# Moving the output sum, the row normalisation and three steps of algebra to other places in the engines' orders

## What is computed

```python
xn = layernorm(x)
# attention: l2-normed Q and K over the rows, all products linear, so a 256x256 matrix per batch
s = xn + gamma * (value_sum + Q^T (K V^T)) * tailor_sum
# feed-forward, every operand in blockwise FP4 (blocks of 16, scale = max|.|/6, rounded to a grid)
gate = fp4(xn) @ fp4(w_gate).T          # 704 wide
y    = fp4(xn) @ fp4(w_up).T
h    = silu(gate) * y
f    = fp4(h) @ fp4(w_down).T
out  = x + s * silu(f)
```

## Time and profile before

| | |
|---|---|
| median of 3 runs | 636.19 us |
| the profiled execution | 638.52 us, span 636.7 us |
| mean granted TensorE clock | 0.973 of full speed |
| DVE busy | 566.0 us (89%) |
| PE busy | 557.4 us (88%) |
| ACT busy | 411.6 us (65%) |
| POOL busy | 273.4 us (43%) |

### The profile page before, as it was taken

The page is one execution under the profiler, slowest core; times in us unless marked ns, Lnnn a source line. Parts: engine busy times, 40 slices in busy tenths (PEclk is TensorE's granted clock), DMA queues, the critical chain, the costliest instruction groups (busy, mean ns, idle before and its releaser), DMA issues.

```text
span 636.7 us, 15147 instructions
## 1 busy us (share of the span) xinstructions
PE 557.4 (88%) x4957; PEld 430.2 (68%) x4957; DVE 566.0 (89%) x1201; ACT 411.6 (65%) x884; POOL 273.4 (43%) x208
## 2 busy tenths in 40 slices
PE   0267879999998998999997979999997999999776
PEld 0244657677786876678785856777885876787655
DVE  6978999989999999999898988989998999877925
ACT  3475788868677777576774767666764875654420
POOL 4453255434424454445535453543644354223216
PEclk9997999999999999999997989999997999999989
DMA  7010000000011011111101111111011110141103
GB/s 235 16 35 16 18 19 18 18 20 18 18 34 34 1 51 51 51 51 51 52 18 34 51 55 52 50 52 51 2 51 50 52 34 34 36 142 42 34 33 150
DMA packets 17474, 29.15 MB, mean 46 GB/s; under 512 B 2673, under 2 KB 4849, under 8 KB 17393
## 3 DMA queue, kind: packets, MB, share of 16 engines
q1 hardware_dynamic: 17392, 28.13, 13.3%
HBM read 19.73 MB, written 8.39 MB: 44 GB/s over the span
## 4 chain that ended last, share of the span: by engine, by line
PE 49%; DVE 30%; issue 12%; ACT 4%; POOL 2%; DVEq 1%; DMA 1%; POOLq 0%; SPq 0%; ACTq 0%
PE GU L1322 22%; PE DS L1332 6%; DVE hg L877 4%; PE G L1389 4%; DVE h L837 3%; PE DS L1334 3%; PE TR L1284 3%; DVE hq L885 3%; DVE xq L826 3%; PE GU L1342 3%; DVE ham L844 3%; DVE y L896 1%; PE TR L1300 1%; PE G L1426 1%; PE G L1404 1%
## 5 line engine op out<-in xcount | busy, mean ns | idle before, releaser
L1322 PE MATMUL GU<-wgu,xqT 128*128 128x352 f16 x1536 | 258.5, 320 | 5.7 <-DVE y L896 3.2
L1322 PEld LDWEIGHTS GU<-wgu,xqT 128*128 128x128 f16 x1536 | 150.2, 100 | 82.1 <-DVE y L896 3.5
L589 ACT ACTIVATE sil<-GU,wkap 128x352 f32<-128x352 f32 x128 | 70.9, 554 | 89.7 <-PE GU L1322 87.2
L514 POOL TENSOR_TENSOR ht<-h,hrr 128x1408 f32<-128x1408 f32 x32 | 82.8, 2589 | 81.6 <-DVE hrr L851 80.0
L837 DVE SCALAR_TENSOR_TENSOR h<-GU,wkap,sil 128x352 f32<-128x352 f32 x128 | 70.1, 547 | 32.4 <-ACT sil L589 26.4
L1332 PE MATMUL DS<-wdT,hqT 128*128 128x256 f16 x704 | 88.5, 275 | 2.6 <-ACT hqT L596 2.6
L480 POOL TENSOR_TENSOR xnat<-xs,xnat 128x510 f16<-128x510 f32 (+1 forms) x32 | 37.0, 1156 | 105.6 <-DVE ht L874 102.9
L487 POOL TENSOR_TENSOR xt<-xs,xrr 128x512 f32<-128x512 f32 x32 | 34.0, 1062 | 100.0 <-DVE hq L885 91.2
L1332 PEld LDWEIGHTS DS<-wdT,hqT 128*128 128x128 f16 x704 | 66.9, 99 | 11.6 <-ACT hqT L596 2.9
L1342 PE MATMUL GU<-Mx,xnT 128*128 128x128 f16 (+1 forms) x648 | 59.7, 234 | 3.1 <-DVE Mx L979 2.4
L885 DVE TENSOR_TENSOR hq<-hg,hs 128x704 f16<-128x704 f16 x128 | 61.0, 519 | 1.0
(11 more groups left out here) (152 smaller groups left out, 973.4 us busy)
## 6 DMA issues: line engine op xcount, KB each, us to landing
xin<-in_L_attn_x SPq DMA_DIRECT2D x34, 256.0 KB, 2.7
xe<-in_L_attn_x SPq DMA_DIRECT2D x25, 256.0 KB, 2.9
out<-o SPq DMA_DIRECT2D x25, 256.0 KB, 2.1
algebra<-in_L_ffn_w_down SPq DMA_DIRECT2D x1, 704.0 KB, 6.9
gring<-in_L_ffn_w_gate SPq DMA_DIRECT2D x1, 640.0 KB, 4.6
gring<-in_L_ffn_w_up SPq DMA_DIRECT2D x1, 640.0 KB, 5.7
xs<-in_L_attn_x SPq DMA_DIRECT2D x2, 256.0 KB, 3.9
xt<-in_L_attn_x SPq DMA_DIRECT2D x2, 256.0 KB, 4.4
```

Source lines behind the costliest of these rows:

```text
L514: g.tensor_tensor(paired(ht[:, 0:2 * I]), paired(h[:, q]), spread(hrr[:, q], 4 * CB), ALU.mult).then_inc(S["ht_d"], 1)
L589: a.activation(sil[:, c], GU[:, c, 0, 0:CH], ACT.Silu, scale=wkap[:, 0:1]).then_inc(S["sil_d"], 1)
L1322: last = t.matmul(GU[:, c, m, 0:CH], xqT[:, k, j, 2 * a_ + kc], wgu[:, b_, kc, 2 * m + c], start=(z == 0 and kc == 0), stop=(z == 2 and kc ...
```

## The change

LAGO = LAGE + 2 makes o and its store run for pair p-12 in iteration p. On POOL, `x_rstd` goes behind `x_divide`. On SP the store goes ahead of the load of xe. On ACT `x_norm` goes from the head of the iteration behind `rows_out(0)`, and `rows_out(0)` from behind `h_abs` to ahead of `h_high`. On DVE xam goes behind the second h and y, both x roundings stand ahead of the hs, and the two squares answers are one, at the later place. The ask "high_low" goes from (4,1,2) to (5,0,0) in all batches but the last.

```diff
+LAGO = LAGE + 2
@@ tables
-                (4, 1, 0): "top", (4, 1, 2): "high_low"}
+                (4, 1, 0): "top", (5, 0, 0): "high_low"}
-        ANSWERS = {... (2, 0, 1): "squares_q", (2, 0, 2): "squares_k", ...
+        ANSWERS = {... (2, 0, 2): "squares", ...
-        ANSWERS_END = {... (1, 1, 1): "squares_q", (1, 1, 2): "squares_k",
+        ANSWERS_END = {... (1, 1, 2): "squares",
@@ drive, active, at_end, end_row
-            for p in range(PAIRS + 1, PAIRS + LAGE + 1):
+            for p in range(PAIRS + 1, PAIRS + LAGO):
-                            h=has(p - LAGH), e=has(p - LAGE), o=has(p - LAGE - 1))
+                            h=has(p - LAGH), e=has(p - LAGE), o=has(p - LAGO))
@@ SP
+                if on["o"]:
+                    e = p - LAGO
+                    wait(sp, "o_d", e + 1)
+                    ko = (k + LAGO) % 2
+                    sp.dma_start(rows(of, e), end_row(p) if at_end(p) else o[:, ko]).then_inc(S[f"out_d{ko}"], 16)
                 if on["e"] and not (isinstance(p, int) and p - LAGE >= PAIRS - ENDS):
                     ke = (k + LAGE) % 2
                     sp.dma_start(xe[:, ke], rows(xf, p - LAGE)).then_inc(S[f"xe_in{ke}"], 16)
-                if on["o"]:
-                    ... the same for p - LAGE - 1
@@ POOL
                 if on["o"]:
-                    e, ko = p - LAGE - 1, (k + LAGE + 1) % 2
+                    e, ko = p - LAGO, (k + LAGO) % 2
                     wait(pool, "y_d", 4 * e + 4)
...
                     x_low(p, k)
+                    if on["mb"]:
+                        wait(pool, "hloq", 2 * p)
+                    x_divide(p, k)
                 if on["xf"]:
                     x_rstd(p + 1)
-                if on["xa"]:
-                    if on["mb"]:
-                        wait(pool, "hloq", 2 * p)
-                    x_divide(p, k)
@@ ACT
-                if on["xa"]:
-                    x_norm(p, k)
                 if on["m"]:
                     silu(p, 0, 0)
...
                     silu(p, 0, 1)
                 attention(0, 1)
+                if on["xt"] and on["m"]:
+                    rows_out(p, k, 0, on["xn"], on["e"])
+                if on["xa"]:
+                    x_norm(p, k)
                 if on["mb"]:
                     h_high(p, k)
                 if on["xf"]:
                     x_stats(p + 1)
                 if on["mb"]:
                     h_abs(p)
-                if on["xt"] and on["m"]:
-                    rows_out(p, k, 0, on["xn"], on["e"])
@@ DVE
                     x_front(p + 1, 1 - k)
-                if on["xa"]:
-                    x_scales(p, k, 0)
...
                     e_mul(p, k, 0)
+                if on["xa"]:
+                    x_scales(p, k, 0)
                 attention(0, 2)
                 if on["xb"]:
                     x_round(p, k, 0)
+                    x_round(p, k, 1)
                 if on["mb"]:
                     h_parts(p, k, 2)
-                if on["xb"]:
-                    x_round(p, k, 1)
```

More of the change, by code:

```diff
@@ L258, in build @@
                 (2, 0, 1): "t1k", (2, 1, 0): "norms", (2, 1, 2): "raw", (3, 0, 2): "tailor", (3, 1, 2): "product",
-                (4, 1, 0): "top", (4, 1, 2): "high_low"}
-        ANSWERS = {(-4, 1, 1): "own_basis", (0, 1, 0): "gram0", (1, 0, 1): "gram1", (1, 1, 0): "turn", (2, 0, 1): "squares_q",
-                   (2, 0, 2): "squares_k", (2, 1, 1): "norms", (3, 1, 0): "tailor", (4, 0, 1): "product", (4, 1, 1): "top",
+                (4, 1, 0): "top", (5, 0, 0): "high_low"}
+        ANSWERS = {(-4, 1, 1): "own_basis", (0, 1, 0): "gram0", (1, 0, 1): "gram1", (1, 1, 0): "turn", (2, 0, 2): "squares",
+                   (2, 1, 1): "norms", (3, 1, 0): "tailor", (4, 0, 1): "product", (4, 1, 1): "top",
                    (5, 0, 1): "high_low"}
@@ L268, in build @@
                     (3, 0, 2): "top", (3, 1, 1): "high_low"}
-        ANSWERS_END = {(0, 0, 2): "gram0", (0, 1, 2): "gram1", (1, 0, 1): "turn", (1, 1, 1): "squares_q", (1, 1, 2): "squares_k",
+        ANSWERS_END = {(0, 0, 2): "gram0", (0, 1, 2): "gram1", (1, 0, 1): "turn", (1, 1, 2): "squares",
                        (2, 0, 1): "norms", (2, 1, 2): "tailor", (3, 0, 1): "product", (3, 1, 0): "top", (4, 1, 2): "high_low"}
@@ L307, in active @@
                 on = dict.fromkeys(("xf", "xa", "xb", "xn", "xt", "m", "mb"), False)
-                return on | dict(h=h_at is not None, e=p - LAGE < PAIRS, o=True)
+                return on | dict(h=h_at is not None, e=p - LAGE < PAIRS, o=p - LAGO < PAIRS)
             if isinstance(p, int):
@@ L311, in active @@
                 return dict(xf=has(p + LEADA + 1), xa=has(p + LEADA), xb=has(p + LEADB), xn=has(p + LEADN), xt=has(p + LEADT), m=has(p), mb=has(p - 1),
-                            h=has(p - LAGH), e=has(p - LAGE), o=has(p - LAGE - 1))
+                            h=has(p - LAGH), e=has(p - LAGE), o=has(p - LAGO))
             return dict.fromkeys(("xf", "xa", "xb", "xn", "xt", "m", "mb", "h", "e", "o"), True)
         def at_end(p):
-            return isinstance(p, int) and p - LAGE - 1 >= PAIRS - ENDS
+            return isinstance(p, int) and p - LAGO >= PAIRS - ENDS
         def end_row(p):
-            return xend[p - (LAGE + 1) - (PAIRS - ENDS)]
+            return xend[p - LAGO - (PAIRS - ENDS)]
         def s_beside(p, j, tail):
@@ L531, in iteration @@
                     x_low(p, k)
-                if on["xf"]:
-                    x_rstd(p + 1)
-                if on["xa"]:
                     if on["mb"]:
@@ L538, in iteration @@
                     x_divide(p, k)
+                if on["xf"]:
+                    x_rstd(p + 1)
                 if i == 2:
@@ L925, in answer @@
                     v.tensor_tensor(Gs[:, :, :], G[:, :].rearrange("p (k n) -> p k n", k=KD), As[:, :, :], ALU.add).then_inc(S["G_ev"], 1)
-                if step == "squares_q":
+                if step == "squares":
                     wait(dve, "tq_ev", b + 1)
                     v.tensor_tensor(prod[:, :, :], t1q[:, :, :], wqT[:, :, :], ALU.mult).then_inc(S["prod_d"], 1)
-                if step == "squares_k":
                     wait(dve, "tk_mm", b + 1)
```

## The result

The changed kernel takes 648.23 us (median of 4 runs, 646.92 to 651.37) against 636.58 us for the kernel before in the same series. The ratio is 1.0186, 95% interval [1.0142, 1.023]. The forecast was 634.6 with a range of 629.0 to 640.5, so the time lies outside, on the side that had a chance of 0.27, and beyond the slow rival (639.7) too. The profiled execution took 647.19 us with a span of 645.4, 8.7 us longer than the span of the earlier trace rows.

The account below looks back on a forecast made before the run. DVE bounds plain iterations, PE those with attention algebra. DVE's lateness summed to -1.6 us, giving 636.9 for the profiled execution; the median, 2.3 below the profiled one, was forecast at 634.6, range 629.0 to 640.5.

Parts of the forecast that it names:

- slow rival: DVE's ht also waits for hT in plain iterations, 13, 18, 21 and 26 among them: 639.5 us, chance 0.23.
- its idle 1.55 takes back 1.55: Iteration 14: DVE's idle time before h absorbs 1.55 us of lateness; with ACT's chain, lateness goes from +4.4 to +3.05.
- the ledger: DVE's lateness added up iteration by iteration against the kernel before; predicted to end at -1.6 us.
- the sum: All predicted gains and losses through iterations and tail: -1.6 us, 636.9 for the profiled execution.
- The idle time of 5 and 6 swallows all of it: First turns: iteration 1 costs 2.7 us, and idle time in 5 and 6 absorbs it, leaving nothing.
- Part 1: POOL's o one pair late: hs gains 1.0 us in 16 iterations, but o may hold the first x rounding, losing 0.9.
- Part 2: POOL's rs and x_shift between xt and the next ht: there is room, and DVE's hss loses nothing.
- the rival of 651 us: DVE's hss waits until POOL's root is over, 0.54 us up to 31 times: +17 us, chance 0.03.
- Part 3: ACT's new order: ht starts no earlier than 5.3 us after the second sil; costs where PE paces, +1.7 in iteration 16.
- Part 4: high_low asked in the next iteration: PE's wait for kap shrinks, -2.8 us each in iterations 18 and 26.
- Part 5: Tail, iteration 32: y waits for o, hs for the second o, delaying ht and kap: +1.5 us.

Follow-up runs that it names:

- gram_early: The changed kernel with DVE's answer gram0 one slot set earlier, at (0,0,2), ahead of both roundings of h; 644.07 us.
- rstd_early: The changed kernel with POOL's x_rstd ahead of x_divide again, as in the kernel before; 647.61 us.
- norm_behind: The changed kernel with x_norm behind h_abs on ACT, and xam and xss behind the first rounding of h on DVE; 657.73 us.
- o_only: The kernel before with only o and its store one pair later and the store ahead of the load of xe; 632.47 us.
- norm_only: The kernel before with only x_norm behind ACT's second sil, xam behind DVE's second h and y, x_rstd behind x_divide; 648.59 us.

## Why the prediction was wrong, point by point

**The step that failed: "its idle 1.55 takes back 1.55" in iteration 14, and the like in 22.** The prediction took the idle time ahead of h as slack of DVE against a PE that has its own time. It gave the condition for this ("a PE that is 2.0 late itself"), and it named a tie for iteration 14 (L1404 waits for G_ev), but it looked for ties behind the idle time and not ahead of it. The tie that counts is L921 to L1389, in the iteration before, and it showed no idle time in the trace because PE and DVE met there within 0.2 us. DVE, then PE, of the kernel before:

```profile
264.87 0.42 DVE L921 SCALAR_TENSOR_TENSOR algebra<-G,algebra 128x256 f32<-128x256 f32 x1
```

```profile
264.64 0.82 PE L1334 MATMUL DS<-wdT,hqT 128*128 128x256 f16 x6
```

The addition ended at 265.29, PE's product ahead of the group at 265.46, and the group began at 265.51. A wait that ends in a tie has length zero and yet carries every lateness over. Cost by gram_early: 1.85 in 14 and 1.26 in 22, 3.1 of the ledger's miss of 10.3.

**The sum of these two iterations was also wrong in itself.** In 14 it goes from +4.4 to +3.05. By its own terms, 1.55 taken back and 1.05 for the chain, it is +3.9: 1.55 us of idle time can't bring a lateness of 4.4 down to PE's 2.0. That step is -0.5, not -1.35, and -0.5 is what gram_early shows. In 22 the sum takes 1.1 back and adds nothing for the chain, though the distance from the second sil to ht was 4.20 us there and 4.22 in 14; by the terms of 14 it is -0.5 too, not -1.1. Together 1.45 us, with which the forecast would have been 636.1. The remaining 0.6 of the miss in 22 has no cause shown.

**"The idle time of 5 and 6 swallows all of it"** failed for another reason. Iteration 1 cost 1.6 by the ledger (2.7 in the sum) and iteration 3 another 0.8, which the sum doesn't have; iteration 5 gave back only 0.2. Its 1.70 us of idle time did vanish, but it had new costs that the prediction priced at nothing: xam waited 0.75 for xs and ht 0.29 for hT, and both products xq took 1.26 us instead of 0.75. And the 0.78 ahead of h in iteration 6 stayed 0.70. DVE of the changed kernel, iteration 5:

```profile
128.02 0.69 DVE L801 TENSOR_REDUCE xam<-xs 128x32 f32<-128x512 f32 x1 [0.75 <-ACT xs L678]
...
130.86 1.62 DVE L874 SCALAR_TENSOR_TENSOR ht<-hT,ht 128x1408 f32<-128x1408 f32 x1 [0.29 <-ACT hT L638]
...
132.67 0.48 DVE L837 SCALAR_TENSOR_TENSOR h<-GU,wkap,sil 128x352 f32<-128x352 f32 x1
133.07 1.26 DVE L826 TENSOR_TENSOR xq<-xg,xs 128x512 f16<-128x512 f16 x2
```

That is the mechanism of the slow rival ("ACT's chain bites in the plain iterations too"), in a place where neither it nor the forecast had it. Cost of iterations 0 to 5: 2.5.

**Part 1, o late: right.** hs takes 0.43 us in every iteration up to the tail (0.44 once), and the first rounding is held by o where the prediction said. Iteration 19 of the changed kernel, DVE and then POOL, against the earlier trace rows:

```profile
376.22 1.28 DVE L817 SCALAR_TENSOR_TENSOR xt<-xT,xt 128x512 f32<-128x512 f32 x1
377.53 0.69 DVE L820 SCALAR_TENSOR_TENSOR xg<-xT,xt 128x512 f16<-128x512 f32 x1
378.14 0.43 DVE L867 SCALAR_TENSOR_TENSOR hs<-hss,hbq,hs 128x44 f16<-128x44 f32 x2
```

```profile
375.67 1.27 POOL L527 TENSOR_TENSOR o<-y,xe 128x512 f32<-128x512 f32 x1
```

Iteration 19 gained 0.18 (predicted 0.1), and 11, 17, 20 and 25 gained 0.75 each (1.0). One row was misread: in the tail's row of hs an o does stand beside it, for its first 0.18 us, and hs takes 0.43 all the same. In iteration 15 of the kernel before hs begins 0.5 us behind the end of o and takes 0.43 too, so the price of 1.0 stands.

**Part 2, the root: right, and the rival of 651 us falls.** In the changed kernel rs runs from 387.62 to 388.33, and hss inside it takes 0.20 us:

```profile
387.62 0.71 POOL L471 TENSOR_TENSOR rs<-ve,half 128x2 f32<-128x2 f32 x1
```

```profile
388.09 0.20 DVE L848 TENSOR_SCALAR hss<-ham 128x88 f32<-128x88 f32 x1
```

rstd_early confirms it. For this pair the trace does not bear out the rule of the Trainium skill's page "SBUF — State Buffer", section "Who interferes with whom", that tensor_scalar can enter a two-port mode and then waits until a POOL instruction that was first ends: in 27 iterations hss begins inside rs and takes at most 0.21 us. Whether hss enters that mode no run shows. In norm_behind a tensor_scalar beside POOL's larger tensor_tensor did wait for its end (384.45 + 0.87 against 384.13 + 1.16), in 28 iterations, and there the trace agrees with the rule.

**Part 3, ACT's chain: right in kind, too small.** Distances of 5.56 us in 14 and 5.67 in 16 stand against the 5.3 and 5.8 worked out. The cost was +2.0, +2.0 and +2.4 in 6, 7 and 8 (predicted 2.2, 1.5, 1.9), and +1.2 and +2.0 in 15 and 16 (1.1 and 1.7), and the same in 23 and 24: 12.8 in all against 11.2. The waits for hT are 0.3 to 0.7 us (1 to 2 were predicted) and are missing in 7, 15 and 23. The larger ones are those of xam for xs, 1.2 us in 14, 1.3 in 15 and 1.75 in 16, as xs ends only 3.2 us after the second sil begins; the sum had priced them in 15 alone. The slow rival's waits in 13, 18, 21 and 26 did not come: no ht waits for hT in 9 to 13, 17 to 21 or 25 to 28.

**Part 4, high_low late: right.** -2.69 and -2.71 in 18 and 26 (predicted 2.8). PE's wait for kap is 0.26 us in iteration 17, and the product behind it runs at full clock (against 3.45 and 3.73 in the earlier trace rows):

```profile
352.80 0.66 PE L1450 MATMUL G<-id,mt 128*128 128x128 f32 x4 [0.26 <-DVE kap L969]
353.30 1.95 PE L1319 MATMUL GU<-wgu,xqT 128*128 128x352 f16 x12
```

**Part 5, the tail: right within 0.5.** y waits for the second o, and kap is late (against the earlier trace rows), DVE and then PE of the changed kernel:

```profile
608.14 0.48 DVE L908 SCALAR_TENSOR_TENSOR y<-GU,unm,gring 128x256 f32<-128x256 f32 x1 [1.77 <-POOL o L527]
```

```profile
613.05 1.12 PE L1450 MATMUL G<-id,mt 128*128 128x128 f32 x4 [4.97 <-DVE kap L969]
```

The tail costs 1.05 (predicted 1.5). How much of it is o's stays open: o_only has +1.9 there, but norm_only, without o late, has +1.2 as well.

**The sum.** By the ledger the miss is 10.3 us in the span: 5.1 in 14 and 22 (3.1 of the tie, 1.45 of the slips in the sum, 0.6 open), 2.5 from iterations 0 to 5, and some 2.7 from sizes of a few tenths each, nearly all on the same side (the tail's 0.5 is on the other). The medians lie 13.6 apart; the other 3.3 come from the step from the profiled execution to the median, which the prediction took as -2.3 and which was +1.0. That the time is so far out is thus in part the luck of the profiled executions, one long before and one short after; with the ledger's miss alone it would be 644.9, outside the range as well.

## What to carry to other kernels

Before idle time is booked as slack that takes back a loss, follow the releaser of the engine that ends it: if that engine has been released by the idle one since the last point at which it ran ahead, the two are tied and nothing is taken back. Such a tie may show no idle time at all; look for a step that starts within 0.2 us of its producer's end, and for a group in a loop that takes longer there than its twin elsewhere. Two insertions into one engine's chain are to be summed before they are compared with the cover, for each may be covered alone and both together not.

## What the runs showed beyond that

A group of products in a loop whose start is held by another engine's result ran 3.6 us instead of 2.76, with single products equally long (324 and 326 ns), where the register instructions between them had no lead. Held there, such a group cost 0.8 us more than the wait itself.

In the two places looked at here, whichever of DVE's rounding and POOL's o began first ran at its own length, and the other was held. In norm_behind, iteration 19, the second x rounding took 1.65 us and POOL's o beside it 1.76 instead of 1.27, while the first rounding, which began 0.05 us ahead of o, took its normal 0.68. In the changed kernel, where o begins 0.55 us ahead of the first rounding (375.67 and 376.22), it is the rounding that is held and o that takes 1.27.
